# A gated graph network in four layers: VectorE's sum moves to the head of the next step, ScalarE's high part and normalising move with it

## What is computed

```python
for l in range(4):
    m = x @ weight[l]
    agg = segment_sum(m[src], dst, num_segments=n_nodes)
    gi = agg @ w_ih.T + b_ih            # three parts: r, z, n
    gh = x @ w_hh.T + b_hh
    r = sigmoid(i_r + h_r)
    z = sigmoid(i_z + h_z)
    n = tanh(i_n + r * h_n)
    x = (1 - z) * n + z * x
out = layernorm(x0 + (x + x0))          # x0: the input
```

## Time and profile before

| | us |
|---|---|
| median of 3 runs | 2386.39 (2386.11 to 2389.70) |
| the profiled execution | 2389.03 |
| its span, first to last instruction | 2387.2 |
| TensorE busy | 2239.4, 94% |
| VectorE busy | 2053.6, 86% |
| ScalarE busy | 1833.7, 77% |
| GpSimd busy | 1689.6, 71% |
| TensorE's mean granted clock | 0.988 |

### The profile page before, as it was taken

The page is one execution under the profiler, slowest core; times in us unless marked ns, Lnnn a source line. Parts: engine busy times, 40 slices in busy tenths (PEclk is TensorE's granted clock), DMA queues, the critical chain, the costliest instruction groups (busy, mean ns, idle before and its releaser), DMA issues.

```text
span 2387.2 us, 48608 instructions
## 1 busy us (share of the span) xinstructions
PE 2239.4 (94%) x11728; PEld 1906.8 (80%) x11728; DVE 2053.6 (86%) x3927; ACT 1833.7 (77%) x3483; POOL 1689.6 (71%) x1654
## 2 busy tenths in 40 slices
PE   3999999999899999999999999999988888988886
PEld 2888888888788888888788888888777777777774
DVE  7788888888688888888688888888779999998987
ACT  1688888888678888888678888888747777777776
POOL 3887777777487777777487777777477777777773
PEclk7999999999999999999999999999999999999998
DMA  2455555555456666666556666656534555554553
GB/s 56 123 160 160 161 160 159 162 157 161 121 162 171 171 171 168 172 172 167 146 146 172 171 167 172 172 167 169 168 100 135 145 142 144 141 145 141 147 142 109
DMA packets 277062, 362.43 MB, mean 152 GB/s; under 512 B 107754, under 2 KB 186586, under 8 KB 276980
## 3 DMA queue, kind: packets, MB, share of 16 engines
q1 hardware_dynamic: 238118, 309.12, 44.0%
q0 software_dynamic: 38784, 52.30, 9.7%
q10 hardware_dynamic: 78, 0.08, 0.0%
HBM read 208.71 MB, written 179.20 MB: 162 GB/s over the span
## 4 chain that ended last, share of the span: by engine, by line
PE 55%; DVE 21%; ACT 12%; issue 8%; DMA 1%; DVEq 1%; POOL 1%; ACTq 0%; POOLq 0%; SPq 0%
PE pZ L852 15%; PE pR L852 7%; PE pHN L852 7%; PE pA L840 7%; DVE diff L1457 4%; PE pO L939 4%; DVE diff L1451 4%; PE pA L852 4%; PE pIN L852 4%; DVE aggT L1414 3%; ACT o_rows L1132 3%; ACT a_hi L1083 3%; PE pR L893 2%; PE pR L896 2%; PE pR L894 2%
## 5 line engine op out<-in xcount | busy, mean ns | idle before, releaser
L688 POOL DMA_INDIRECT gath<-state,idx x900 | 932.7, 1036 | 267.0 <-issue 251.7
L665 POOL TENSOR_TENSOR h_lo<-hT,h_hi 128x250 fp32r<-128x250 f32 (+2 forms) x400 | 345.9, 865 | 286.2 <-DVE diff L1457 282.9
L1083 ACT CAST a_hi<-aggT 128x500 fp32r<-128x500 f32 x396 | 241.9, 611 | 330.8 <-DVE aggT L1414 330.8
L688 POOL DMA_INDIRECT gath<-in_x_dram,idx x300 | 320.4, 1068 | 101.8 <-issue 71.1
L1457 DVE TENSOR_TENSOR diff<-pZ,diff 128x500 f32<-128x500 f32 x400 | 271.4, 678 | 40.7 <-issue 0.5
L1096 ACT ACTIVATE rg<-pR,bsum 128x500 f32<-128x500 f32 x400 | 270.3, 676 | 44.2 <-PE pR L896 26.8
L1405 DVE TENSOR_TENSOR a_lo<-aggT,a_hi 128x500 fp32r<-128x500 f32 x396 | 269.1, 680 | 5.4 <-ACT a_hi L1083 4.7
L1078 ACT CAST sel<-sel 128x504 fp32r (+1 forms) x400 | 244.2, 611 | 31.7 <-DVE flag_i L1388 29.6
L1414 DVE TENSOR_TENSOR aggT<-pA,hT 128x500 f32<-128x500 f32 x396 | 264.9, 669 | 3.3 <-PE pA L840 3.3
L1108 ACT ACTIVATE pZ<-pZ,bsum 128x500 f32<-128x500 f32 x400 | 257.4, 643 | 9.4 <-PE pZ L852 9.4
L852 PE MATMUL pZ<-a_hi,wf_hi 128*128 128x500 f32 x400 | 190.7, 477 | 66.2 <-DVE diff L1457 66.0
(11 more groups left out here) (215 smaller groups left out, 6323.1 us busy)
## 6 DMA issues: line engine op xcount, KB each, us to landing
columns<-newT SPq DMA_DIRECT2D x300, 250.0 KB, 2.7
hT<-columns SPq DMA_DIRECT2D x300, 250.0 KB, 2.7
state<-o_rows SPq DMA_DIRECT2D x300, 224.0 KB
x_rows<-in_x_dram SPq DMA_DIRECT2D x200, 224.0 KB
out_dram<-o_rows SPq DMA_DIRECT2D x91, 224.0 KB
gath<-state,idx POOLq DMA_INDIRECT x900, 2.5
state<-o_rows SPq DMA_DIRECT2D x297, 26.0 KB
idx<-edge_src SPq DMA_DIRECT2D x395, 1.5 KB
```

The source lines that it names most:

```text
L665: nc.gpsimd.tensor_tensor(part_of(h_lo, u)[:, cols], hT[:, u % RING, cols], part_of(h_hi, u)[:, cols].bitcast(F32), ALU.subtract).then_inc ...
L688: pool.indirect_dma_start(out=gath[:, u % RING, j, :], out_offset=None, in_=states[l], in_offset=bass.IndirectOffsetOnAxis(ap=idx[:, u % R ...
L1083: nc.scalar.copy(by_rows(a_hi[:, u % RING, :]), sums_of if summed else by_rows(aggT[:, :])).then_inc(s_ahi, 1)
```

## The change

In a step, VectorE first makes the sum of block b+1, ahead of difference, product and new state of block b-1; before, it made the sum of block b+2 behind r times hn. The low part of the same block stays late in the step. ScalarE takes the high part right behind tanh of block b-1 and ahead of the r gate, where it stood ahead of the z gate. What stood ahead of the r gate is divided: in layers 1 to 3 the high part of the state (`high`) stays ahead and the rows out (`rows`) go behind the r gate; in layer 0 the rows stay ahead and the two copies of `high` go behind. The four normalising instructions of layer 3 are one group behind the r gate and the widening and ahead of the z gate. The ramp's fourth step no longer makes the sum and parts of block 5. GpSimd's, TensorE's and SyncE's orders are the same.

The core of the diff:

```diff
--- before.py
+++ after.py
@@ ScalarE, step @@
                         if not ramp:
+                            if exists(i, u, 1):
+                                high_part(l, *after(i, u, 1)[:2])
+                            if l:
+                                high()
+                            else:
+                                rows(i, u)
+                        r_gate(l, b, u, first and l == 0)
+                        if ramp and u == 3:
+                            high_part(l, 4, 4)
+                        if ramp or l:
                             rows(i, u)
-                            high()
-                        fresh = half_done(i, u, OUTLAG) if final else None
-                        if not fresh:
-                            normal(i, u, 0)
-                        r_gate(l, b, u, first and l == 0)
-                        if fresh:
-                            normal(i, u, 0)
-                        if ramp:
-                            if u == 3:
-                                high_part(l, 4, 4)
-                            rows(i, u)
+                        if ramp or l == 0:
                             high()
...
+                        normal(i, u)
                         if not seeded(i, u):
                             n_gate(u, l * ADDED_APART + b + 1)
                         if ramp and u < 3:
                             high_part(l, *after(i, u, 1)[:2])
-                        if not ramp and exists(i, u, 2):
-                            high_part(l, *after(i, u, 2)[:2])
                         z_gate(l, b, u)
-                        normal(i, u, 1)
...
@@ VectorE, step @@
+                        if not ramp and exists(i, u, 1):
+                            aggregate(l, *after(i, u, 1)[:2])
                         if exists_before(i, u, ADDED_APART + 1):
                             difference(l, *after(i, u, -1)[:2])
                             product(l, *after(i, u, -1)[:2])
...
-                        summed = after(i, u, 1 if ramp else 2)[:2] if exists(i, u, 2) else None
-                        if summed and not (ramp and u == 3):
+                        summed = after(i, u, 1)[:2] if exists(i, u, 1) and not (ramp and u == 3) else None
+                        if ramp and summed:
                             aggregate(l, *summed)
...
-                        if summed and not (ramp and u == 3):
+                        if summed:
                             low_part(l, *summed)
-                        if ramp and u == 3:
-                            aggregate(l, 5, 5)
```

## The result

The changed kernel takes 2402.95 us, the median of 5 runs (2401.38 to 2407.98), beside 2388.57 for the kernel before on the same chip. By the medians it is 14 us slower, and the ratio of the means is 1.0067, with a 95% interval of 1.0052 to 1.0082. The forecast was 2397. The profiled execution took 2407.98 us, its span is 2406.1 us, TensorE's mean granted clock 0.986. The sum of the prediction was nearly right because its loss in layer 0 and its gains in the other layers were both put too small.

What follows compares the result with a forecast made beforehand. TensorE bounds layer 0, two equal chains layers 1 and 2, a chain through ScalarE layer 3. 2389.0 + 32 - 13 - 5 - 1 = 2402, 2399 against the median, lowered to 2397 us for a possibly shorter h_lo; range 2364 to 2412.

Steps and rivals of the forecast that it cites:

- layer 0's term: Layer 0: late h_lo on GpSimd holds VectorE's select each step, 86 x 0.37 = 32 us more.
- the two causes named for the gain: Layer 3: earlier sum with its high part, and normalising joined ahead of the z gate, cut the chain; 13 us less.
- The r gate starts at 405.85 ... and it cannot move: Layer 0: the r gate starts just after the last R matmul ends and stays there after the change.
- Layer 0 is caught worse: Rival, layer 0: h_lo holds g_lo, VectorE's step is 6.41 us, 67 us lost, 2432 us; chance 0.08.
- which the slower step itself undoes: Layer 0 rival's condition: h_lo must fall behind select each time, which the slower step was said to undo.
- The forecast's own chain: Layer 0: chain from one z group through h_hi, h_lo and held select to z two steps on, 6.00 us a step.
- Layers 1 and 2, 5 us forecast: Layers 1 and 2: product comes earlier, leaving TensorE as bound; at most 0.06 us a step, 5 us less.
- Layer 3, 13 us forecast: Layer 3: chain through ScalarE cut, VectorE's own work bounds, ten steps 61.3 us against 62.8; 13 us less.
- no wait of the high part: Sign expected in layer 3's new trace: ScalarE's high part no longer waits, as its sum was made earlier.
- GpSimd does not get in: Rival, layer 0: h_lo runs beside sum and difference, period stays 5.63, 2367 us in all; chance 0.18.
- The wait costs nothing: Rival: the wait between a_lo and sum is free, helping layers 3 and 0; 2373 us; chance 0.10.
- Layer 3 gives nothing: Rival, layer 3: late GpSimd instructions hold VectorE in more than two steps in ten; 2410 us; chance 0.04.

Runs made afterwards that it cites:

- e1_high_first_l0: The changed kernel, but in layer 0 the copies hT and h_hi stay ahead of the r gate and the rows go behind it; 2351.31 us.
- e2_short_h_lo_l0: The changed kernel, but from block 20 on GpSimd makes only 100 of the 500 columns of layer 0's h_lo; 2350.69 us, one run.
- e7_normalise_alone: The kernel before, with only the four normalising instructions joined ahead of the z gate and every sum in its old place; 2358.82 us.
- e10_rows_ahead_l1_l2: e5_two_sums with rows_out of layers 1 and 2 back ahead of hT's high part and the r gate; 2341.21 us, one run.
- e3_high_part_late_l0: The changed kernel, but layer 0's high part goes back behind the widening and ahead of the z gate; 2381.85 us, one run.
- e5_two_sums: e1_high_first_l0 with the sum in two buffers by turns, so it waits only for the low part before the last; 2341.93 us.

## Why the prediction was right, and where it was wrong

The forecast was slower, by layer 0's h_lo beside VectorE, against gains in the other layers. In this outline it is so; e1_high_first_l0 and e2_short_h_lo_l0 show the first half, e7_normalise_alone and e10_rows_ahead_l1_l2 the second. But the chain from which layer 0's term was added up is not the one that the layer runs by, and in layer 3 one of the two causes named for the gain brings none.

- **Layer 0, 32 us forecast, 51.6 measured.** The failed step is "The r gate starts at 405.85 ... and it cannot move". It was tied to the end of the R matmul. But the change puts the high part ahead of it on ScalarE's queue, and the high part waits for a sum that is now made late in VectorE's row. From the sum at 402.49 the two ways run beside each other: 0.71, 0.52, 0.47, 0.58, 0.45 and 0.69 to h_lo (405.91), and 0.59, 0.77, 0.79, 0.59 and 0.65 to the select (405.88). Nothing moves one against the other. So the rival "Layer 0 is caught worse", to which I gave 0.08, was the case, and its condition, "which the slower step itself undoes", was wrong: the phase hangs on the sum, which slows down with the step. Its price of 6.41 was near (6.22; it had 0.07 too much for the wait between low part and sum, and 0.1 more in the steps up to low part). The forecast's own chain was sized well, in part by luck: 6.00 against 5.99 in e3_high_part_late_l0.
- **Layers 1 and 2, 5 us forecast, 17 measured.** The mechanism holds, the size doesn't. I took the gap of 0.17 from one place and let 0.06 be the whole gain. Over 60 blocks of layer 1 (780 to 1100 us) the gap falls from 0.134 to 0.111, and the distance from the first to the second Z matmul from 0.328 to 0.261: 0.090 together, and the period fell by 0.091. A first matmul that has waited takes longer until the next starts, and that stood in the length of 0.49 in the earlier trace rows. This is read from the rows, not tested by itself.
- **Layer 3, 13 us forecast, 17 measured.** 60.8 us in ten steps against 61.3. The plain step is 5.84, not 5.91: the wait between low part and sum costs 0.12 in it, not the 0.19 of the earlier trace rows, and e5_two_sums confirms its size. The size came out, but only one of the two reasons given: the joined normalising brings the gain, and the early sum costs 0.09 a step beside it (the square under e7_normalise_alone). Its sign "no wait of the high part" did not come: the high part waits 75.3 us over 70 steps for the sum, 1.08 each, which costs nothing there because r times hn never waits for the r gate. It is the same wait that the prediction overlooked in layer 0. VectorE's h_lo in the step behind the square root is held 0.4 to 0.5 instead of 0.3.
- **The other rivals.** "GpSimd does not get in": it gets in behind the select each time. "The wait costs nothing": it costs 9.4 us by e5_two_sums. "Layer 3 gives nothing": it gave 17.
- **The sum.** Term by term, 52 - 17 - 17 makes 18 more, against 19 between the profiled executions (2407.98 and 2389.03) and 14 between the medians. The prediction's terms made 13, and its last step took off some more, to 2397. It was near by luck: layer 0's error of 20 us is nearly offset by the 16 of the others. With the other terms as forecast, layer 0's 52 us would have made it 33 more than before, 2419 from the median of 2386, outside the range.

## What to carry to other kernels

Before an instruction's time is called fixed, look at everything that now stands ahead of it on its engine and at what each of those waits for: a wait moved to the head of a queue ties the whole rest of the step to its releaser. Try the parts of a change one by one: here the joined normalising gained, the early sum gained in two layers and lost in one, and two copies behind the r gate cost more than all the rest brought. Where VectorE and GpSimd both work on SBUF, put a VectorE instruction that reads PSUM beside GpSimd's.

## What the hardware showed that was not expected

- The hold between VectorE and GpSimd works both ways and passes on instruction by instruction. In the changed kernel GpSimd's h_lo, 0.03 us behind the select in the step shown, takes a mean of 1680 ns instead of 1186, and then holds g_lo (1539 instead of 551), though VectorE's instructions stand in a row without a pause. Nearly always whoever starts first is not held, and the edge is sharp. In all 88 steps of the changed kernel in which the select starts before h_lo or at most 0.01 us behind it, h_lo is held; in e3_high_part_late_l0 the select is held in every step in which it starts 0.02 to 0.74 us behind h_lo. The Trainium skill, SBUF — State Buffer, "Who interferes with whom", says that issue order decides; these traces agree, but the recorded starts do not settle every case: the select of the earlier trace rows started 0.18 ahead of h_lo and was held, and so was one in e3_high_part_late_l0 (0.19 ahead, at 119.93).
- Where a VectorE instruction waits for the one directly in front and only overwrites what that reads, the wait costs 0.11 to 0.12 us in most steps (0.70 against 0.59) and 0.27 to 0.39 in some three of ten in layer 0 (0.86 to 0.98 against 0.59); the mean there is 0.17.
- A first Z matmul that had to wait is followed by the next after 0.33 us instead of 0.26 (means over 60 blocks of layer 1, before and after the change).
